# Constant matmuls in four of TensorE's waits, in a GNN, attention and FFN kernel on one core

## The reference, cut to what matters

```python
xn = layernorm(x)
h = prelu(xn @ lin_W.T + lin_b, lin_a)
for l in range(2):                                   # graph layers
    h = h + segment_sum(h[src], dst)                 # aggregation
    h = prelu(h @ W1[l].T + b1[l], a[l])             # "up"
    h = h @ W2[l].T + b2[l]                          # "down"
    h = relu(batchnorm(h))                           # statistics over all 1250 nodes
x = x + h + linear_attention(xn)
x2 = layernorm(x)
g = mean(relu(x2 @ gfc1.T + b) @ gfc2.T + b2)        # gate: 8 numbers
W1m, W2m = W1 + sum(g[e] * tv_W1[e]), W2 + sum(g[e] * tv_W2[e])
y = x2 + relu(x2 @ W1m.T + b1m) @ W2m.T + b2m        # ffn1, ffn2
out = x + layernorm(y) * lng + lnb
```

## Time and profile before

| | |
|---|---|
| three runs | 568.98, 569.9, 569.6 us; median 569.6 |
| the profiled execution | 569.8 us, of which 568.0 us from the first to the last instruction |
| TensorE matmuls busy | 500.9 us (88%) |
| VectorE, ScalarE, GpSimd busy | 347.9, 231.2, 178.2 us |
| TensorE's share of the chain that ended last | 65% (VectorE 18%, ScalarE 7%) |
| mean granted TensorE clock | 0.945 of full speed |

### The profile page before, as it was taken

The page is one execution under the profiler, slowest core; times in us unless marked ns, Lnnn a source line. Parts: engine busy times, 40 slices in busy tenths (PEclk is TensorE's granted clock), DMA queues, the critical chain, the costliest instruction groups (busy, mean ns, idle before and its releaser), DMA issues.

```text
span 568.0 us, 11565 instructions
## 1 busy us (share of the span) xinstructions
PE 500.9 (88%) x3909; PEld 390.3 (69%) x3909; DVE 347.9 (61%) x732; ACT 231.2 (41%) x519; POOL 178.2 (31%) x151
## 2 busy tenths in 40 slices
PE   3988899998999799999999967999999789898960
PEld 2776688765556666789988956899889579765420
DVE  4679988597976466462375543214754656279493
ACT  4744222743223511225355365211563486533231
POOL 1564400031930400207955400002453042124174
PEclk9998799999989999999999979899999769999785
DMA  8502200020200100010000200000302670000022
GB/s 248 156 2 74 75 1 3 1 74 1 76 1 1 76 2 1 6 72 0 0 1 1 74 0 3 2 0 0 129 0 77 258 333 2 1 2 0 0 94 86
DMA packets 5006, 27.45 MB, mean 48 GB/s; under 512 B 796, under 2 KB 921, under 8 KB 3304
## 3 DMA queue, kind: packets, MB, share of 16 engines
q1 hardware_dynamic: 4968, 26.92, 13.6%
HBM read 24.36 MB, written 2.56 MB: 47 GB/s over the span
## 4 chain that ended last, share of the span: by engine, by line
PE 65%; DVE 18%; ACT 7%; issue 5%; POOL 1%; DMA 1%; DVEq 0%; ACTq 0%; SPq 0%
PE ps L452 38%; PE ps L597 15%; PE ps L439 4%; PE ps L506 3%; PE ps L496 2%; DVE stage L1428 2%; DVE stat L1090 1%; DVE r L1068 1%; PE ps L436 1%; PE ps L706 1%; DVE late L1069 1%; DVE r L1140 1%; ACT r L917 1%; ACT late L834 1%; POOL late L1535 1%
## 5 line engine op out<-in xcount | busy, mean ns | idle before, releaser
L452 PE MATMUL ps<-late,wslot 128*128 x960 | 104.8, 269 | 1.0 <-ACT ohs L891 0.8
L452 PE MATMUL ps<-r,wslot 128*128 128x250 f16 x840 | 100.6, 281 | 5.1 <-DVE r L1068 5.0
L452 PEld LDWEIGHTS ps<-late,wslot 128*128 128x128 f16 x960 | 92.1, 97 | 13.5 <-issue 3.5
L1544 POOL TENSOR_TENSOR wslot<-stage,wslot 128x2048 f16<-128x2048 f32 x9 | 36.9, 4102 | 203.4 <-ACT wslot L749 126.2
L452 PEld LDWEIGHTS ps<-r,wslot 128*128 128x128 f16 x840 | 84.6, 101 | 18.9 <-DVE r L1068 6.6
L597 PE MATMUL ps<-late,r 125*128 (+1 forms) x800 | 90.1, 274 | 4.8 <-issue 3.7
L597 PEld LDWEIGHTS ps<-late,r 125*128 125x128 f16 x800 | 78.5, 99 | 14.7 <-issue 5.8
L452 PE MATMUL ps<-wslot,r 128*125 128x512 f16 x300 | 75.6, 404 | 2.6 <-DVE late L1069 2.6
L1069 DVE SCALAR_TENSOR_TENSOR late<-ps,late 128x250 f32 (+2 forms) x60 | 29.3, 503 | 62.6 <-ACT late L924 55.3
L452 PEld LDWEIGHTS ps<-wslot,r 128*125 128x125 f16 (+1 forms) x300 | 41.2, 144 | 28.8 <-issue 6.8
L756 ACT ACTIVATE late<-ps 125x500 f16<-125x500 f32 (+1 forms) x25 | 14.7, 587 | 100.0 <-PE ps L439 100.0
(11 more groups left out here) (169 smaller groups left out, 708.2 us busy)
## 6 DMA issues: line engine op xcount, KB each, us to landing
late<-in_tv SPq DMA_DIRECT2D x2, 4096.0 KB, 17.5
out<-r SPq DMA_DIRECT2D x10, 250.0 KB
x<-in_x SPq DMA_DIRECT2D x5, 448.0 KB
stage<-in_w_up SPq DMA_DIRECT2D x2, 1024.0 KB, 5.2
stage<-in_w_down SPq DMA_DIRECT2D x2, 1024.0 KB, 4.7
stage<-in_w_lin SPq DMA_DIRECT2D x1, 1024.0 KB, 6.4
stage<-in_w_k SPq DMA_DIRECT2D x1, 1024.0 KB, 6.0
stage<-in_w_q SPq DMA_DIRECT2D x1, 1024.0 KB, 4.8
```

The lines of the kernel that those rows point to most:

```text
L452: last = nc.tensor.matmul(out, stat_(hs, b), mov(hm, b), start=start and n == 0, stop=stop and n == 3 * blocks - 1)
L1544: nc.gpsimd.tensor_tensor(wslot[:, i % SLOTS, 1].rearrange("p k n -> p (k n)"), stage[:, :], wslot[:, i % SLOTS, 0].rearrange("p k n -> p ...
```

## The change

A helper `spin` writes matmuls of `ones` by `ident` into a given bank; nobody reads the result, and nobody is signalled. It is called in four places: ahead of the first transposes (10 matmuls into bank 7), behind each layer's last down product (12 into bank 6, in both layers), and ahead of ffn2 (14 into bank 7). At the last place a wait for the first of the two `b2_ready` counts stands ahead of it.

```diff
+            def spin(bank_, times):
+
+                for _ in range(times):
+                    nc.tensor.matmul(ps[:, bank_, 0:128], ones[:, :], ident[:, :], start=True, stop=True)
+
...
+            spin(7, 10)
             flip_pair(0)
...
                 transposed(f"down{layer}", weight(f"down{layer}"), a_t,
                            ready=lambda j: pe.wait_ge(tmp_free, KB + 20 * layer + KB * j + KB))
+                spin(6, 12)
...
             pe.wait_ge(wm_split, FB + 2)
+            pe.wait_ge(b2_ready, 1)
+            spin(7, 14)
             pe.wait_ge(b2_ready, 2)
             natural("ffn2", hid_t, w2m, blocks=FB, ready=lambda i: pe.wait_ge(tmp_free, KB + 2 * KB * J + J + i + 1),
```

## The result

The changed kernel takes 572.9 us (median of 20 runs, 567.7 to 576.8), the kernel before 569.5 us beside it (20 runs, 568.3 to 571.5); the ratio is 1.005, interval 1.0033 to 1.0068. It is slower, by some 3 us, and 572.9 lies outside the range. A second timing gave 572.45 us (12 runs), ratio 1.0058 [1.0032, 1.0085].

What follows compares the result with a forecast made beforehand. TensorE, 65% of the chain that ended last, was taken to lose time at its lower clock level after waits. Terms -0.3 - 0.5 + 0 + 1.2 = +0.4 us gave 570.0 us against the median, range 568.2 to 572.0.

Steps and rivals of the forecast that it cites:

- opening: Spin ahead of the first transposes: cost hidden, clock rises but falls again before the products; -0.3 us.
- behind down0: Spin behind the first layer's last down product: cost hidden, clock falls later, ScalarE's loop gains; -0.5 us.
- behind down1: Spin behind the second layer's last down product: cost hidden, low clock there stays as before; 0 us.
- ahead of ffn2: Last spin, behind the late wait for `wm_split`, delays ffn2 and then VectorE; +1.2 us.
- tail: After ffn2's first tiles: VectorE's 0.61 us wait for the tenth tile may go or not; 0 us.
- same: Whole kernel: the parts nearly cancel, 570.0 us, within 568.5 to 570.7; chance 0.48.
- they come late: Rival behind down1: row sums come late because the clock falls before 447.3; +1.1, 571.1 us, chance 0.08.
- the middle case: Ahead of ffn2: clock falls at 526.0 and rises after about 3.4 us of solid work; +0.8 us.
- the low case: Ahead of ffn2: clock stays low until 532.7 as before; +2.5 us.
- decides if the last spin starts before the clock falls: Rival: clock held where it should be, -0.7 ahead of ffn2, -1.1 behind down0, -0.6 opening; 567.2 us, chance 0.14.
- The spins do nothing to the clock: Rival: no gain in opening or behind down0, last spin delays ffn2 at low clock, +2.5; 572.1 us, chance 0.22.
- The opening gave no more: Rival: clock stays up from the opening's spin into the products, -2.6; 567.7 us, half of it 568.9, chance 0.08.

Runs made afterwards that it cites:

- e9_dead40: Kernel before plus 10 products (40 instructions) in a branch that isn't taken, nothing more executed: 571.76 us against 570.0, ratio 1.0034.
- e1_tiny: Changed kernel with each spin product cut to 2 columns and 1 row of output, as many instructions: 570.65 us, ratio 1.0014.
- e2_wide: Changed kernel with the same spin columns in products of 512 columns, 52 added instructions in place of 192: 570.56 us, ratio 1.0012.
- e6_pad: Changed kernel plus 216 instructions in a branch that isn't taken, ahead of the first aggregation: 576.15 us, ratio 1.0105.
- e11: Changed kernel repeated without edit, one profile: 573.2 us.
- e12: Changed kernel repeated without edit, one profile: 570.1 us.
- e17: Changed kernel repeated without edit, one profile: 572.8 us.
- e5: Changed kernel repeated without edit, timed and profiled: 572.45 us over 12 runs, ratio 1.0058; 568.3 us in its profile.
- e8: Changed kernel repeated without edit, one profile: 568.9 us.
- e18: Changed kernel repeated without edit, one profile: 574.7 us.
- e4_no_last: Changed kernel without the spin ahead of ffn2, keeping those of the opening and behind both layers: 570.1 us, ratio 1.0002.
- after: The first profile of the changed kernel, no further edit: 570.6 us.
- e15_before: Kernel before repeated without edit, one profile: 570.2 us.
- e16: Kernel before with only one spin of 14 products, ahead of the wait for the merged W2: 567.0 us against 569.8, ratio 0.9951.
- e7: Changed kernel with the last spin and its wait put ahead of the wait for the merged W2: 568.94 us, ratio 0.9975.

## Why the prediction was wrong

By its steps, with what the profiles showed: the mean of the changed kernel's seven less the mean of the four of before, whose first is the zero of the table (us).

```
step                                predicted (bounds)    by the profiles
opening                             -0.3  (-2.6 to 0)      -0.5
elsewhere ahead of 240              no term                +0.15
first aggregation (where code lies) no term                +2.05
behind down0                        -0.5  (-1.1 to 0)      -0.9
behind down1                         0    (-1.9 to +1.1)    0
ahead of ffn2                       +1.2  (-0.7 to +2.5)   +1.6
tail                                 0    (-0.6 to 0)      -0.35
sum                                 +0.4                   +2.05
```

**The step that failed is the sum itself: it had no term for where TensorE's code lies.** "Nothing is removed or moved" was read as a statement on work, and each record was priced where it runs. But 192 instructions also push all code behind them along, and the 40 of the opening, the only ones ahead of the first aggregation, are enough to open a gap of 1.95 us there. e9_dead40 shows it without any work, by its time and by its profile; e1_tiny shows that the changed kernel's gap stays without the spins' columns; e2_wide that the gap moves by as many instructions as are left out ahead of it; e6_pad that with 256 ahead it is at the jump itself. Without this term the measured steps sum to 0.0, and "same" would have stood by the profiles. It doesn't fill the whole miss: with +2.05 the forecast is 572.05, just outside the range, and 0.8 us are left to the measured 572.9 (see what stays open). The Trainium skill ("Runtime: NRT & Kernel Launch", section "Instruction fetch mechanics") says that code is brought in blocks of 16 KiB, and that a taken branch to a place outside what is loaded has to wait for the transfer. e6_pad agrees, with 5.27 us at the jump. In the changed kernel and in e9_dead40 the jump itself takes 0.36 and 0.45 us and the gap comes 19 products behind it, in code without a jump, at the same 5 us after it. That the code behind the gap is the next block, asked for only by the jump, is the reading that fits all of these; no row names the block.

**Opening (cost right, gain right in some executions only).** The spin ran from 2.64 to 7.2 us, at the lower price, and cost nothing: TensorE still waited 1.07 us for the first tile. In the first profile the clock rose ahead of the eight transposes (1.35 us against 1.92) and fell again at 10.9, as forecast, so the products still took 5.58 of the 6.61 us. e11 has 1.35 us too, e12 1.51 and e17 1.80; but in e5, e8 and e18 the transposes took 1.93 us, as without a spin, and no fall is recorded behind them. There the spin did nothing to the clock. This is e5:

```profile
8.13 1.93 PE L501 MATMUL ps<-ident,late 125*128 125x125 f32 x8 [0.88 <-ACT late L782]
```

The difference at 19.4 lies between -1.67 and -0.20 in the changed kernel and between -1.21 and +0.17 in eight profiles without these columns, four of them of before: the two overlap, and so the -0.5 of the means can't be told from nothing. (In e4_no_last, with the same spin, it is +1.32: the products waited until 14.19.)

**Behind down0 (right in mechanism, low in size).** In six of seven profiles the fall at 334.8 is gone, not late, and ScalarE's loop gains 1.03 us there, nearly the whole bound; in the seventh, e17, it comes at 340.3 and the gain is 0.18. In three of the seven (after, e11, e18) about 1 us of it is given back by 360: behind a wait at 350 to 355, which before has too (the second layer's jump: 3.69 us before, 3.40 us in the changed kernel), the clock falls and stays low longer (0.62, 0.50 and 0.59 over 356 to 360, against 0.70 before, and 0.97 and 0.90 in e5 and e8, which keep the gain).

**Behind down1 (right in its term).** The spin and the row sums ended ahead of VectorE, which started L1400 in order; the rival that they come late is out. The clock was low for 10 us in place of 17, where the prediction had it low as before, and no step between 444 and 464 moved: there the path goes through VectorE and the transfers (DMA share about 1).

**Ahead of ffn2 (mechanism right, term too small by 0.4).** The path was read rightly: the spin begins behind the late wait, at 524.95, not inside it. Its first 1.35 us lie at the higher level and 3.4 us at the lower, as in the middle case, and both tiles behind it run at full speed. The measured +1.2, in all seven against the first profile of before, equals the forecast by luck. The middle case, which is what ran, was priced at +0.8; spin and tiles took some 0.2 us more each than its sum had. The quarter of the way to the low case, which filled this, stood for a clock that stays low, and it never did. What was missed is the other side. Without a spin that stretch takes 1.4 us less in four of seven profiles (e15_before, e1, e4, e9), because the low stretch is sometimes shorter. Against the mean of before the term is 1.6. The case that "decides if the last spin starts before the clock falls" was named as a rival, at the wrong price: it needs the spin ahead of the wait, and is then worth -3.05.

**The tail.** VectorE's wait of 0.61 us at the tenth tile went away in five of seven.

**Two readings that were off.** TensorE's busy time was to grow by 10 to 15 us, by the price of the spins; it grew by 7.1, as the 15.3 us of spins were partly won back where other instructions ran at the higher level. And the list of low stretches before left out the one from 58.0 to 64.8 (granted clock 0.50).

**The same by medians.** One early spin gives -2.8 us (e16); with the other spins and their code it is -0.6 (e7), so these cost 2.2; late in place of early costs 3.5 (e5, +2.95 in the same comparison as e7), where the profiles have 4.25. By the profiles' steps the other spins and their code cost 0.65 (2.05 for the gap, less 0.9 and 0.5), so some 1.5 us of the 2.2 are without a cause here as well.

**The rivals.** "The spins do nothing to the clock" had the nearest time (572.1), by a mechanism that the rows rule out as a whole: behind both layers and ahead of ffn2 the clock moved, in the opening in four of seven profiles. The opening gave no more than forecast, the row sums were not late, and the clock was not held ahead of ffn2; it is with e16's order.

**What stays open.** The seven profiles of the changed kernel lie 2.05 us above the four of before, the timed medians 2.95 to 3.4. Of its 32 runs in the two timings 25 are above 570.7, of the seven profiled ones three. The collision of L1068 with L1553 came in two of seven profiles of the changed kernel, in none of four of before and in none of the nine other kernels. Both came on one chip, on which no other kernel was profiled, so the chip is a rival that nothing here excludes. The collision adds about 2 us to an execution, and would have to come in most of the timed runs to fill the difference. Whether the change brings it about, and by which shift, no run isolates. On the one chip where both kernels were profiled, the changed one is no slower (568.3 and 568.9 against 569.5, 568.1 and 570.2), though its 12 timed runs there gave 572.45 against 569.5. So the timings have 0.9 to 1.3 us more of slowdown than the profiles, and its cause is open.

## What to carry to other kernels

Price the code as well as the work: after adding instructions to an engine's straight code, look in the timeline for a new wait on "issue" behind the engine's jumps, in places that weren't edited, and put unexecuted instructions into the kernel before to price it alone. A spin that should hold the clock belongs right behind the work that precedes the wait, ahead of every wait that comes late; behind it, it is plain delay, here 4.2 us apart for the same 14 products. When one profile shows less than the timings do, take several and compare them stretch by stretch; the steps that repeat in every one (the last spin's to 0.01 us, the gap's within 0.4 us in six of seven) are the change's, and the others tell what the spread is made of.

## What was unexpected of the hardware

- 40 instructions that never run cost 1.8 us; with 216 of them in the changed kernel TensorE stood 5.50 us, at another place, in place of 1.95. In either case work went on 4.8 to 5.3 us after the same jump.
- The second layer's jump takes 3.3 to 3.8 us in every profile, 3.69 us in the kernel before, and TensorE stands meanwhile: that was there before any edit.
- An f32 product of 128 columns is two matmuls: 24 of them took 2.85 us at the higher level, 20 took 4.61 at the lower; as wide products the same columns cost the same ahead of ffn2 (+1.15 and +1.20).
- One VectorE compare took 4.60 us in place of 0.83 when it started 0.13 us behind a GpSimd instruction of 4.05 us.
- A higher mean clock (0.957 against 0.945) came with a slower kernel: the clock is worth only what the path does at that time.
